# A Perceiver block kernel: the first head pair's keys and scores are spread over the projection loop, and a slot's values come right behind its transposes

## What is computed

```
xn    = LN(x)                                   # 256 x 512
for each of 16 heads h:
    q   = xn @ Wq[h].T                          # 256 x 128    (p1)
    q   = q @ w_kc_q[h]                         # 256 x 384    (p2)
    q   = q * cos + rotate_half(q) * sin        #              (rotation)
    qr  = q @ W_qr[h]                           # 256 x 64     (p3)
    key = rope(ctx) @ W_kr[h]                   # 4096 x 64    (keys)
    s   = qr @ key.T                            # 256 x 4096   (scores)
    p   = exp(s - rowmax(s))
    c   = p @ rope(ctx)                         # 256 x 128    (turn, weigh)
    v   = (c @ w_kc_kv[h].T) / rowsum(p)        # 256 x 128    (values)
    x  += v @ Wo[:, h].T                        #              (head_out)
# beside it, for the feed-forward block that comes later:
w_int = round(w / (max|w row| / 127))           # 15 jobs of weight rows
```

## Time and profile before

| | us |
|---|---|
| median of three runs (lowest, highest) | 1141.03 (1140.18, 1143.40) |
| the profiled execution, its own time | 1141.82 |
| its span in the profile | 1140.1 |
| TensorE busy, matmuls | 1046.1 (92%) |
| VectorE busy | 722.3 (63%) |
| ScalarE busy | 571.0 (50%) |
| GpSimd busy | 268.1 (24%) |

### The profile page before, as it was taken

The page is one execution under the profiler, slowest core; times in us unless marked ns, Lnnn a source line. Parts: engine busy times, 40 slices in busy tenths (PEclk is TensorE's granted clock), DMA queues, the critical chain, the costliest instruction groups (busy, mean ns, idle before and its releaser), DMA issues.

```text
span 1140.1 us, 18082 instructions
## 1 busy us (share of the span) xinstructions
PE 1046.1 (92%) x6823; PEld 819.1 (72%) x6823; DVE 722.3 (63%) x1313; ACT 571.0 (50%) x1099; POOL 268.1 (24%) x209
## 2 busy tenths in 40 slices
PE   7989999999987985599999999999899999899996
PEld 5545889999975752377787778778777878676843
DVE  3655465565544874378777777877777885463635
ACT  3344444544432210356766666676666669443323
POOL 6800244443423000121111212111111110103512
PEclk9999999999998995689999999999999999989998
DMA  9450266566322420101111020111103026223010
GB/s 281 99 212 1 68 234 240 205 222 239 121 77 75 130 82 24 29 4 27 31 52 31 27 56 1 52 31 52 38 17 84 1 62 139 68 74 152 1 60 18
DMA packets 72249, 97.45 MB, mean 85 GB/s; under 512 B 35665, under 2 KB 53233, under 8 KB 71026
## 3 DMA queue, kind: packets, MB, share of 16 engines
q1 hardware_dynamic: 72178, 96.49, 26.8%
HBM read 91.58 MB, written 4.90 MB: 85 GB/s over the span
## 4 chain that ended last, share of the span: by engine, by line
PE 74%; DVE 9%; POOL 5%; issue 5%; DMA 3%; ACT 3%; SPq 0%; DVEq 0%; POOLq 0%; ACTq 0%
PE PS L1549 12%; PE PS L1412 11%; PE PS L1526 9%; PE PS L1538 7%; PE PS L1431 5%; PE PS L1499 4%; DVE scores L1074 3%; PE PS L1563 2%; PE PS L1470 2%; PE PS L1479 2%; PE PS L1260 2%; PE PS L1618 2%; DMA xn<-in_w 2%; PE PS L1701 1%; PE PS L1627 1%
## 5 line engine op out<-in xcount | busy, mean ns | idle before, releaser
L1074 DVE TENSOR_SCALAR_CACHE_REDUCE scores<-PS 128x512 f32<-128x512 f32 x256 | 167.3, 687 | 89.7 <-PE PS L1526 88.5
L778 ACT ACTIVATE scores<-scores,nmX 128x512 f32<-128x512 f32 x256 | 182.1, 716 | 56.1 <-DVE nmX L1078 56.1
L1120 DVE TENSOR_TENSOR pL<-PS,pH 128x1024 fp32r<-128x1024 f32 x128 | 155.7, 1217 | 28.5 <-ACT pH L801 28.5
L801 ACT ACTIVATE pH<-PS 128x1024 fp32r<-128x1024 f32 x128 | 131.2, 1025 | 83.4 <-PE PS L1538 83.3
L1549 PE MATMUL PS<-pH,kvH 128*128 128x256 f32 x512 | 160.5, 314 | 5.2 <-DVE pL L1120 5.0
L1549 PE MATMUL PS<-pH,kvL 128*128 128x256 f32 x512 | 143.7, 281 | 0.0
L1549 PE MATMUL PS<-pL,kvH 128*128 128x256 f32 x512 | 143.6, 280 | 0.0
L1538 PE MATMUL PS<-ident,scores 128*128 128x128 f32 x1024 | 133.3, 275 | 0.8 <-ACT scores L778 0.8
L1538 PEld LDWEIGHTS PS<-ident,scores 128*128 128x128 f32 x1024 | 116.4, 142 | 2.7 <-ACT scores L778 1.8
L1549 PEld LDWEIGHTS PS<-pH,kvH 128*128 128x128 f32 x512 | 96.8, 189 | 29.5 <-issue 14.6
L1526 PE MATMUL PS<-keyH,qsH 64*128 64x512 f32 x256 | 68.3, 530 | 40.0 <-DVE scores L1074 40.0
(11 more groups left out here) (309 smaller groups left out, 2282.0 us busy)
## 6 DMA issues: line engine op xcount, KB each, us to landing
rawG<-in_wg SPq DMA_DIRECT2D x16, 768.0 KB, 5.5
rawU<-in_wu SPq DMA_DIRECT2D x16, 768.0 KB, 7.0
rawD<-in_wd SPq DMA_DIRECT2D x16, 768.0 KB, 6.3
xn<-in_w SPq DMA_DIRECT2D x11, 512.0 KB, 4.1
wblk<-blocks SPq DMA_DIRECT2D x4, 1056.0 KB, 8.0
wb<-w_rows SPq DMA_DIRECT2D x32, 128.0 KB, 3.3
wqX<-in_wqX SPq DMA_DIRECT2D x16, 256.0 KB, 2.6
woX<-in_woX SPq DMA_DIRECT2D x8, 512.0 KB, 4.0
```

What stands on the lines that cost most here:

```text
L778: act.activation(at, at, ACT.Exp, bias=nmX[:, p % 2, h, q:q + 1], accum_out=csum[:, p % 2, NT * h + q, c:c + 1]).then_inc(exp_done, 1)
L801: act.activation(pH[:, j % 2], PS[:, 2 + 2 * (j % 2):4 + 2 * (j % 2), :].rearrange("p k (h t) -> p (k h) t", t=T), ACT.Copy).then_inc(pH_r ...
L1074: dve.tensor_scalar(sp_[:, h, q, c * CH:(c + 1) * CH], PS[:, h, :], 1.0, None, ALU.mult, ALU.max, accum_out=cmax[:, h, q, c:c + 1]).then_i ...
L1120: dve.tensor_tensor(pL[:, j % 2], PS[:, 2 + 2 * (j % 2):4 + 2 * (j % 2), :].rearrange("p k (h t) -> p (k h) t", t=T), pH[:, j % 2].bitcast ...
```

## The change

The projection loop takes over the first pair's keys and scores. Keys come in heads 1 to 5 (`KEYS_AT`), in banks 7 and 1 by turns. A head n in `AHEAD` has a score between `p1(n + 1)` and `p3`/`p2(n)`, and VectorE copies it ahead of `rotated(n)`; a head in `BEHIND` has one after `p2(n)`, copied after `rotated(n)`. These scores use banks 1 and 7, and `p1` bank 0 alone. `keys(1, 0)` and ten filler matmuls stand ahead of the last `p3`. The scores' buffers therefore exist in the projections already; `wqX` moves to the place of the later `wint1`, `wqr` into `xn`, and `qm1` is dropped, its product going into `qb` in place. In the loop over pairs `weigh(p, j - 1)` stands right behind `turn(p, j)`; VectorE makes `pL` first in each slot; ScalarE makes `keyH` after the `exps`. `row_max(2p)` now stands in slots 2 and 3 of pair p, `row_max(2p + 1)` in slots 12 and 14. GpSimd does `low_parts` ahead of `round_rows`, and SyncE loads the next `wkr` ahead of its wait for the rounding.

```diff
+KEYS_AT = {1: (0,), 2: (1, 2), 3: (3, 4), 4: (5, 6), 5: (7,)}
+AHEAD = {7: 2, 9: 5, 11: 8, 13: 11, 14: 13, 15: 15}
+BEHIND = {5: 0, 6: 1, 7: 3, 8: 4, 9: 6, 10: 7, 11: 9, 12: 10, 13: 12, 14: 14}
...
+        keys_room = sb("keys_room", [P, 2 * L], F32, early)
+        wqX = sb("wqX", [P, 2, KT, XK], F32, early)
...
+        sp_ = A("scores", [P, 2, NT, L])
+        cmax = A("cmax", [P, 2, NT, NCH]); nmX = A("nmX", [P, 2, 2, NT]); csum = A("csum", [P, 2, 2 * NT, NCH]); recX = A("recX", [P, 2, 2 * NT])
         both = arena
         arena = ExitStack()
-        wqX = A("wqX", [P, 2, KT, XK]); kcq = A("kcq", [P, 2, XQ]); wqr = A("wqr", [P, 4, QT, XR])
+        kcq = A("kcq", [P, 2, XQ]); wqr = xn[:].rearrange("p t d -> p (t d)")[:, 0:4 * QT * XR].rearrange("p (h k n) -> p h k n", h=4, k=QT)
         cosQ = A("cosQ", [P, QT, T]); sinQ = A("sinQ", [P, QT, T])
-        qh = A("qh", [P, 2, T]); qm1 = A("qm1", [P, QT, T]); qm2 = A("qm2", [P, QT, T]); qb = A("qb", [P, 4, QT, T])
+        qh = A("qh", [P, 2, T]); qm2 = A("qm2", [P, QT, T]); qb = A("qb", [P, 4, QT, T])
...
+            sp.dma_start(wkr[:], a["wkr"][0:2].rearrange("m p n -> p m n")).then_inc(wkr_in, 16)
+            sp.wait_ge(xnT_ps, 4 * NT)
             for m in range(2):
...
+                if p + 2 < XP:
+                    sp.wait_ge(wkrL_ready, p + 1)
+                    sp.dma_start(wkr[:, p % 2], a["wkr"][p + 2]).then_inc(wkr_in, 16)
...
-                round_rows(n)
                 if n % 2 == 0 and n // 2 + 2 < XP:
                     low_parts(n // 2 + 2)
+                round_rows(n)
...
-                act.activation(qh[:, n % 2], PS[:, n % 2, 0:T], ACT.Copy).then_inc(qh_ready, 1)
-                if n % 2 and n >= 5:
-                    ranks_out((n - 5) // 2)
-                    if (n - 5) // 2 < 2:
-                        high_query((n - 5) // 2)
-                if n % 2 == 0 and n:
-                    high_keys(0, n // 2 - 1)
+                act.activation(qh[:, n % 2], PS[:, 0, 0:T], ACT.Copy).then_inc(qh_ready, 1)
+                for c in KEYS_AT.get(n - 1, ()):
+                    high_keys(0, c, 1 if c % 2 else 7)
+                if n % 2 == 0 and n >= 4:
+                    ranks_out((n - 4) // 2)
+                    if (n - 4) // 2 < 2:
+                        high_query((n - 4) // 2)
             ranks_out(XP - 2)
-            high_keys(0, NCH - 1)
-            ranks_out(XP - 1)
...
+            first_exps(0)
+            ranks_out(XP - 1)
...
-                    if j % 2 and j + 1 < SLOTS and p + 1 < XP:
-                        high_keys(p + 1, (j + 1) // 2)
-                    if j == SLOTS - 2 and p + 2 < XP:
-                        high_keys(p + 2, 0)
                     if j == 6 and p + 2 < XP:
                         high_parts(p + 2)
                         high_query(p + 2)
                     if j + 2 < SLOTS:
                         for q in range(NT):
                             exps(p, j % 2, q, j // 2 + 1)
+                    if j % 2 and j + 1 < SLOTS and p + 1 < XP:
+                        high_keys(p + 1, (j + 1) // 2)
+                    if j == SLOTS - 2 and p + 2 < XP:
+                        high_keys(p + 2, 0)
...
-                dve.tensor_tensor(qm1[:], big[:, 0:QT], cosQ[:], ALU.mult)
+                wait(dve, p3_done, (n - 4) // 2 + 1)
+                dve.tensor_tensor(qb[:, n % 4], big[:, 0:QT], cosQ[:], ALU.mult)
...
-                dve.tensor_tensor(qb[:, n % 4], qm1[:], qm2[:], ALU.add).then_inc(qb_ready, 1)
-
-            def low_keys(p, c):
+                dve.tensor_tensor(qb[:, n % 4], qb[:, n % 4], qm2[:], ALU.add).then_inc(qb_ready, 1)
...
-            for s in range(SLOTS):
-                scores_out(0, s)
-                if s == 2:
-                    low_keys(1, 0)
-            for half in range(2):
-                row_max(0, half)
+            for n in range(XH):
+                if n in AHEAD:
+                    scores_out(0, AHEAD[n], (1, 7))
+                rotated(n)
+                for c in KEYS_AT.get(n, ()):
+                    low_keys(0, c, 1 if c % 2 else 7)
+                if n in BEHIND:
+                    scores_out(0, BEHIND[n], (1, 7))
+            low_keys(1, 0)
             for p in range(XP):
                 for j in range(SLOTS):
+                    dve.wait_ge(pH_ready, SLOTS * p + j + 1)
+                    dve.tensor_tensor(pL[:, j % 2], PS[:, 2 + 2 * (j % 2):4 + 2 * (j % 2), :].rearrange("p k (h t) -> p (k h) t", t=T),
+                                      pH[:, j % 2].bitcast(F32), ALU.subtract).then_inc(pL_ready, 1)
                     if j and p + 1 < XP:
                         scores_out(p + 1, j - 1)
                     if p and j in (4, 6, 8, 10):
                         add_out(p - 1, (j - 4) // 4, (j - 4) // 2 % 2, 7)
                     if j % 2 and j + 1 < SLOTS and p + 1 < XP:
                         low_keys(p + 1, (j + 1) // 2)
-                    dve.wait_ge(pH_ready, SLOTS * p + j + 1)
-                    dve.tensor_tensor(pL[:, j % 2], PS[:, 2 + 2 * (j % 2):4 + 2 * (j % 2), :].rearrange("p k (h t) -> p (k h) t", t=T),
-                                      pH[:, j % 2].bitcast(F32), ALU.subtract).then_inc(pL_ready, 1)
                     if j == SLOTS - 2 and p + 2 < XP:
                         low_keys(p + 2, 0)
-                    if p + 1 < XP and j in (0, 2):
-                        row_max(2 * p + 1, j // 2)
+                    if j in (2, 3):
+                        row_max(2 * p, j - 2)
                     if p + 1 < XP and j in (12, 14):
-                        row_max(2 * p + 2, (j - 12) // 2)
+                        row_max(2 * p + 1, (j - 12) // 2)
...
-                wait(pe, qh_ready, n - 1)
+                wait(pe, qh_ready, n)
                 for kt in range(KT):
-                    mm = pe.matmul(PS[:, b, 0:T], wqX[:, b, kt, :], xnT[:, kt, :], start=(kt == 0), stop=(kt == KT - 1))
+                    mm = pe.matmul(PS[:, 0, 0:T], wqX[:, b, kt, :], xnT[:, kt, :], start=(kt == 0), stop=(kt == KT - 1))
...
-            for s in range(SLOTS):
-                scores(0, s)
-                if s == 1:
-                    wait(pe, keyL_ready, NCH)
-                    keys(1, 0)
+            for n in range(XH):
+                if n + 1 < XH:
+                    p1(n + 1, (n + 1) // 2, (n + 1) % 2)
+                if n in AHEAD:
+                    scores(0, AHEAD[n], (1, 7))
+                if n % 2 and n >= 3:
+                    p3((n - 3) // 2)
+                p2(n, n // 2, n % 2)
+                for c in KEYS_AT.get(n, ()):
+                    wait(pe, keyL_ready, c - 1)
+                    keys(0, c, 1 if c % 2 else 7)
+                if n in BEHIND:
+                    pe.wait_ge(keyL_ready, NCH)
+                    scores(0, BEHIND[n], (1, 7))
+            pe.wait_ge(sX_out, 2 * SLOTS)
+            keys(1, 0)
+            stay_awake(10, 0)
+            p3(XP - 1)
             for p in range(XP):
                 more = p + 1 < XP
                 for j in range(SLOTS):
                     turn(p, j)
+                    if j:
+                        weigh(p, j - 1)
                     if j and more:
                         scores(p + 1, j - 1)
                     if p and j == 2:
@@ -1589,8 +1597,6 @@
                             pe.wait_ge(vX_ready, p - (j < 3))
                             wait(pe, oX_added, 4 * (p - 1) + min(max((j - 3) // 2, 0), 4))
                         keys(p + 1, (j + 1) // 2)
-                    if j:
-                        weigh(p, j - 1)
                     if j == SLOTS - 2 and p + 2 < XP:
                         pe.wait_ge(keyL_ready, (p + 2) * NCH)
                         keys(p + 2, 0)
```

More of the change, by code:

```diff
@@ L382, in _ @@
                     sp.dma_start(sinQ[:], a["sinQ"]).then_inc(qtab_in, 16)
+            sp.dma_start(wkr[:], a["wkr"][0:2].rearrange("m p n -> p m n")).then_inc(wkr_in, 16)
+            sp.wait_ge(xnT_ps, 4 * NT)
             for m in range(2):
                 load_rank(m)
-            sp.dma_start(wkr[:], a["wkr"][0:2].rearrange("m p n -> p m n")).then_inc(wkr_in, 16)
             for n in range(XH):
@@ L427, in _ @@
                 store_rows(2 * p)
-                if p + 2 < XP:
-                    sp.wait_ge(wkrL_ready, p + 1)
-                    sp.dma_start(wkr[:, p % 2], a["wkr"][p + 2]).then_inc(wkr_in, 16)
                 if p + 1 == XP:
@@ L748, in high_query, with high_keys @@
                 act.activation(qsH[:, p % 2], qr[:, p], ACT.Copy).then_inc(qsH_ready, 1)
-            def high_keys(p, c):
+            def high_keys(p, c, bank=7):
                 act.wait_ge(key_ps, p * NCH + c + 1)
                 wait(act, sX_ps, (p - 1) * SLOTS + 2 * c + 2)
-                act.activation(keyH[:, c * CH:(c + 1) * CH], PS[:, 7, :], ACT.Copy).then_inc(keyH_ready, 1)
+                act.activation(keyH[:, c * CH:(c + 1) * CH], PS[:, bank, :], ACT.Copy).then_inc(keyH_ready, 1)
             def ranks_out(m):
```

(33 more changed lines are left out.)

5 lines of the change are left out of this document (2 added, 3 removed).

## The result

The changed kernel takes **1146.18 us** (median of 20 runs, 1141.54 to 1150.07); the kernel before, run beside it on the same chip, 1142.08 (20 runs, 1135.89 to 1146.45). The ratio is 1.004, its 95% interval 1.0026 to 1.0055: slower by 0.4%, a little over the 0.3% that counts as a difference here. The prediction was 1129 us and faster; the time lies outside its range. The profiled execution took 1146.48 us, with a span of 1144.8. TensorE is busy 1050.7 us (1046.1 before), VectorE 731.2 (722.3), ScalarE 571.4, GpSimd 269.4: nothing in these totals shows where the time went.

A forecast was written before the change was run, and what follows sets the result against it. TensorE was taken to bound the kernel, with losses in projections, scores-only stage and loop start. -16.2 + 4.1 = -12.1 from the profiled 1141.82 gives 1129.7; the median being 0.8 lower, 1129 us, range 1117 to 1142.

The forecast's parts named there:

- Part 1: Projections to the loop's start: spread keys and scores and no row_max stall bring turn(3) of pair 0 16.2 us earlier.
- the charge for the clock: Projections, behind the 3.8 us wait at head 5: score 0 and head 6 at the lower level, about 2.5 us.
- about 110 us between p2(0) and turn(0): Projections to pair 0's start: a distance in the trace that would show the forecast right.
- Two banks, no second buffer: Scores-only stage before the loop: matmuls and VectorE's copies follow one another, some 3.1 us a score.
- Part 2: Order within the loop's slots: same matmuls, bounds -10 to +11 us over 112 slots, taken as 0.
- Part 3: Changes of pair: old waits 2.3, new 3.5; +0.6 us each, six times, and 0.8 into pair 7: 4 us lost.
- the stretch with a change of pair, with idle pieces of 0.43 and 1.48 us, kept 1.00: Change of pair in the kernel before: full granted clock despite idle pieces, cited against a clock fall in heads 7 to 15.
- In pair 7 no scores run; head outputs only change places, 0 +- 2: Last pair, slots without scores: the new order leaves its time unchanged, within 2 us.
- The clock falls in the mixed stage: Rival, heads 7 to 15: short TensorE waits drop the clock to the lower level, +23 us, 1152 us; chance 0.11.
- The slot order costs: Rival, loop slots: a late pL or dearer step behind scores, 0.1 us in each of 112, +11, 1140 us; chance 0.11.
- The loops gain too: Rival, changes of pair: the idle 2.3 us at seven changes go instead of growing, 1109 us, halfway 1119; chance 0.15.

The follow-up runs named there:

- e6: Changed kernel with filler matmuls in three waits of the projections (30 behind p1(0), 14 before the first score, 12 before the score ahead of head 15): 1139.33 us.
- e9: Kernel before with only the first pair's keys and scores spread into the projections; old slot order, old places of the row maxima: 1144.98 us.
- e7: Kernel before with only the new places of the row maxima, and GpSimd and the queue in the new order: 1121.73 us.
- e10: Kernel before with the row maxima's new places and five filler matmuls ahead of each first-pair score but the first; nothing spread: 1109.41 us.
- e1: Changed kernel with the old order within a slot on TensorE, VectorE and ScalarE; the rest of the change stays: 1119.02 us.
- e4: Changed kernel with six filler matmuls in TensorE's wait between scores(14) and scores(15): 1137.44 us.
- e5: Changed kernel with weigh last in the slot again, in the last pair only: 1141.69 us.
- e2: Kernel before with only the new order within a slot: 1156.63 us.
- e8: Changed kernel with both the old slot order of e1 and the projection fillers of e6: 1109.94 us.

## Why the prediction was wrong

**Part 1 gives 16.2 us: 12.9.** The order of events was right: a score and its neighbours in turn, 13.4 and 13.3 us for two heads (416.48, 429.88, 443.21) where the text had 13.6, the first score behind a wait of 3.63 (3.6), the wait for the row maxima gone, 1.5 before weigh(0) (1.7). From turn(0) to turn(3) it forecast 10.0 us and 10.1 were measured. The miss lies ahead of turn(0): 110.7 us behind the first copy by the forecast, 113.9 measured. The step that failed is the charge for the clock: 2.5 us, once, behind the wait at head 5. The clock fell behind the waits of 2.06 and 4.02 us as well (rows above), and p2(0) came 4.1 us behind the first copy for 3.6. With three waits filled, e6 reached 118.8, against the forecast's 120.7 on the same mark. The sign "about 110 us between p2(0) and turn(0)" came true with 109.8, but by luck: the times in the text are 464.2 - 357.1 = 107.1.

The reading of what the gain was is the larger fault. I took the scores-only stage for a loss that spreading removes. By e9 the spreading alone, with `wqr` in `xn`, gains nothing, by e7 the rows' places alone gain 8.9 at the start, and only behind these is the spreading worth 4.3 on the mark (128.0 to 123.7) and 2.7 in the medians. "Two banks, no second buffer" was a true reading of the earlier trace rows, but most of the price was the clock (0.57), which e10 buys back with fillers.

**Part 2, the slots: 0, and right.** 7.43 us for two. From turn(3) to turn(15), where only the body runs, the second pair takes 48.9 us in the changed kernel (545.9 to 594.8), 48.9 in e1 and 48.7 before.

**Part 3, the change of pair: 4.1 us lost, and 17 measured.** The waits were foreseen well (1.75 for 1.8, 1.50 for 1.7). Where no clock fell, the change of pair took 18.5 and 18.9 us, for 18.3. Two steps failed. The first: all durations were those of the upper level, since "the stretch with a change of pair, with idle pieces of 0.43 and 1.48 us, kept 1.00". That stretch did not stand for the new one: behind the wait of 1.75 the clock fell in five of seven, for 1.5 us each, and e4 shows it by filling that wait alone. Of the 11.6 us in the periods 6.0 are the clock's; 5.6 are left for the waits. The forecast had 0.6 a change for them, though its own figures give 18.3 - 17.5 = 0.8, or by the waits 3.5 - 2.3 - 0.19 = 1.0; over the six changes these come to some 5 or 6 us.

The second: "In pair 7 no scores run; head outputs only change places, 0 +- 2", with 0.8 for the way into it. It was +5.6. Without scores, two slots hold 5.44 us of TensorE's work, just over the loop of turn, high part, low part and `weigh` (0.89 + 1.04 + 1.24 + 1.69, 4.9 with the steps between). The head output of 0.86 us, which had stood ahead of `weigh` and hidden that latency, now stands behind it and lies in the loop: 5.79, three times. The slots with `values` and the first head output lost more, 0.5 and 1.4, the latter with a wait of weigh(3) of 1.10 for pL(3). e5 gives 2.9 of it all back; the rest is the dearer change of pair.

**The sum.** The forecast -16.2 + 4.1 = -12.1; the marks say -12.9 + 11.6 + 5.6 = +4.3. The forecast compared new waits with old ones and set the rows' gain against them, 1.48 a change. e7 shows that gain as 1.7 a change; e2 shows that under the new order nothing of it is left. Against a kernel with the rows' places (e1), the order costs 20.6 us in the periods (four changes at 4 us and two at 2.5 and 2.3) and 5.1 in the last pair.

**The rivals.** None was it as written. "The clock falls in the mixed stage" had the right mechanism in the wrong place: that stage kept 0.93 from 424 to 470 us, with two of the falls of Part 1 in it. "The slot order costs" looked for its price in each of 112 slots, and it lay at the ends: in two slots of sixteen, and in the pair without scores. "The loops gain too" was right about the `row_max` waits, as e7 shows, and its counter-argument, two scores back to back on the same banks at the end of a pair, names the wait behind which the clock then fell. The Trainium skill (TensorE: Matmul & The Clock Gate, "A second HAM failure mode: psum-queue depth-cycling"), which says that frequent short idles between matmul groups make the clock swing, was weighed against one stretch of the kernel before and set aside. The scores-only stage (0.57) is the nearest case of it here. At the changes of pair the clock swung too, to 0.79 over 8 us, but behind one wait in some 69 us.

## What to carry to other kernels

When a matmul group moves, look at the ends of the loop and at the pass without a successor first: ask of each pair of neighbours what had covered the hand-over between them (here weigh between two scores on the same banks), since the body may have slack and the ends none. Price a new wait of TensorE twice, as the wait and as what runs behind it at the lower clock; a few filler matmuls tell the two apart in one run and were worth as much as a rewritten schedule. Before work is moved to shorten a stage, test whether what stands at its end isn't a round trip of its own: here the row maxima's places alone gave 20 us, and the spreading without them nothing.

## What the hardware showed beside this

The length of a wait alone does not say whether the clock falls. In the changed kernel the same wait of 1.75 us with the same work around it dropped it at 526, 595, 731 and 800 us and left it at 1.00 at 664; one of 2.15 at 869 left it, one of 2.00 at 936 dropped it. In the four kernels with this change of pair and no fill in it (the changed one, e2, e5, e6) it fell in 20 of 28. In the kernel before it never fell at a change of pair, though TensorE waited up to 2.19 us in one piece there:

```profile
816.50 0.50 PE L1526 MATMUL PS<-keyH,qsH 64*128 64x512 f32 x2 [2.19 <-DVE scores L1074]
```

In the projections the clock fell behind the wait of 2.06 us in the six kernels in which the wait of 3.63 ahead of it was empty, and in neither of the two in which that one was filled (e6, e8). So a wait's price has to be taken over several passes, with what stands ahead of it.

After the wait of 9.84 us p1(1) took 3.75 us for eight matmuls, and with 30 fillers in it 3.24, with 3.70 us left empty at the end of the wait. And what precedes the change scattered by more than some of the effects: ScalarE's first `qh` copy came between 350.6 and 357.9 us in thirteen profiles; whether the spread kernels' being on the late side (six of eight behind 353.9) is more than chance is open.
